# Attention fused with two graph layers on one core: scores behind the outputs, fill between the outputs' parts, and half of the output sum ahead of the maximum

## Chip, cores and metric

One core of a Trainium2 chip runs the whole program. The metric is device time in microseconds, the median of several runs. Engines: PE is TensorE (PEld its weight load), DVE is VectorE, ACT is ScalarE, POOL is GpSimd, SP is SyncE, which issues the DMAs.

## What is computed

The input is x of 32 batches of 512 x 512 and a matrix adj of 512 x 512 with about 3% nonzero entries. Two layers follow each other, each with a layernorm over a residual:

```python
# layer 0
y = einsum('nm,bmd->bnd', adj, x)
x = layernorm(x + y @ weight + bias)
# layer 1: 8 heads of 64, masked by adj == 0
q, k, v = split(x @ w_qkv)
attn = softmax(where(adj == 0, -inf, (q @ k.T) * scale))
o = (attn @ v) @ w_proj + b_proj
x = layernorm(x + (o + (layernorm(o) * ln_gamma + ln_beta)))
```

All is float32. The kernel splits each operand into a rounded high part and the rest (`_hi`, `_lo`) and multiplies hi by hi, hi by lo and lo by hi, so a product costs three matmuls.

## The kernel before

The program has two stages. Layer 0 runs first for all 32 batches and leaves its result in DRAM. The attention stage then runs batch after batch; this is where the change is. A batch has 16 steps (`STEPS`), numbered k. Four steps in a row form a pair: two heads (`PAIRS` is 4), each step handling 128 of the 512 query rows of both heads. A pair's number is also called group.

The scores of step k go through this chain. PE computes them (`scores`, L800) into two banks. DVE adds the mask and finds the row maximum (`masked_max`, L1114). ACT takes the exponent and the row sums (`exponent`, L1013). DVE takes the reciprocal (`inverse`, L1123). POOL multiplies (`normalise`, L728 and L731). PE turns the probabilities in 16 transposes (`turn`, L816). ACT copies the result as pt_hi (L1020) and DVE subtracts to get pt_lo (L1131). This chain is spread over several steps: around the turn of step k, DVE takes the reciprocal for k+1 and the maximum for k+2, ACT the exponent for k+2, POOL normalises k+1, and PE makes the scores of k+3.

When the four steps of a pair are turned, PE multiplies them with v. This is `attend_v` (L840), in four parts of eight matmuls: pt_hi run 0, pt_hi run 1, pt_lo run 1, pt_lo run 0. Each run needs the end of the one before it on the same banks (`pv_half`). The two output banks hold their halves on different partitions, so ACT copies one part of them (`ot_halves`, L1036 and L1037) and DVE adds the other (`ot_sum`, L1149, two instructions on 64 partitions each, the first on partitions 0 to 63). These run in the first step of the next pair.

PE's time between these is filled with other products in units of two simultaneous matmuls (`qk_matmuls`, `v_matmuls`, `project`: L849 and L851). A pair has 48 units. `EARLY` says how many of the next pair's units are issued already in this pair's third step (the first number) and fourth step (the others); `FILL` gives, for the first three steps, the units ahead of the scores and behind them. Pair 0 fills with v, pair 1 with the projection of the batch before, pairs 2 and 3 with q and k of the next batch. Units 24 to 47 of each pair write the output banks, `g_bank[2]` and `g_bank[3]`, which are `o_bank`: unit 24 stands right behind the turn of the second step and waits for both instructions of `ot_sum` (`ot_summed`, L876, L897, L917).

Every engine works its instructions off in the order in which the program lists them. `ready_to_turn` (L805) is PE's wait for the normalised probabilities of the next step and for the pt_lo that frees the turn's banks. In the first three steps it stands ahead of the last fill unit; at the end of a pair it stands ahead of the last matmuls of the last output part.

POOL and ACT also handle the rows of the finished batch at fixed steps (`O_STEP`, `Z_STEP`, `S_STEP`): ACT's `scaled` (L1049) and `result` (L1054), POOL's `scale` (L749), `add_z` (L753, L756) and `power` (L737), DVE's statistics (L1157 to L1162) and `row_shift` (L1167).

Of the kernel before, what the change touches and what calls it, by code (L numbers as in the profile page):

```python
# [31 lines left out]
def graph_layers(nc, x, adj, w0, b0, wqkv, wproj, bproj, gamma, beta, out):  # L32
    B, N, D = x.shape
    T = N // P
    HEAD = 64
    PAIRS = D // (2 * HEAD)
# [15 lines left out]
    with ExitStack() as whole:  # L52
# [483 lines left out]
        with ExitStack() as second:  # L536
# [13 lines left out]
            pt_lo = sb("pt_lo", [P, 2, T, N], F32R)  # L550
# [26 lines left out]
            STEPS = PAIRS * T  # L577
# [59 lines left out]
            S_STEP = [9, 11, 13, 15]  # L637


            EARLY = (4, 6, 2)  # L640
            FILL = ((8, 4), (12, 4), (8, 0))
            assert sum(EARLY) == 12 and sum(EARLY) + sum(map(sum, FILL)) == 48
            BEFORE = [sum(EARLY) + sum(map(sum, FILL[:n])) for n in range(T - 1)]
            assert BEFORE[1] + FILL[1][0] == 36
# [140 lines left out]

            @block.tensor
            def _(pe):
                def scores(b, k):

                    pair, n = k // T % PAIRS, k % T  # L790
                    if n == 0:
                        pe.wait_ge(qklo_made, (b + k // STEPS) * 8 + (2 * pair + 2))
                    parts = ((q_hi, k_hi), (q_hi, k_lo), (q_lo, k_hi))

                    if not (isinstance(b, int) and b * STEPS + k == 0):
                        pe.wait_ge(max_found, b * 32 + 2 * k)
                    for i, (l, r) in enumerate(parts):
                        for a in range(2):
                            h = slice(a * HEAD, (a + 1) * HEAD)
                            last = pe.matmul(s_bank[a][:], l[h, pair, n * P:(n + 1) * P], r[h, pair, :],  # L800
                                             start=i == 0, stop=i == 2)
                            if i == 2:
                                last.then_inc(scores_made, 1)
# [14 lines left out]
                                if a == 1 and m == T - 1:  # L818
                                    last.then_inc(probs_turned, 1)

                def attend_v(b, p, part, run):

                    first, end = part is pt_hi and run == 0, part is pt_lo and run == 0
                    if part is pt_hi and run == 0:
                        pe.wait_ge(pthi_made, b * 32 + (8 * p + 8))
                    elif part is pt_hi:
                        pe.wait_ge(pv_half, b * 16 + (4 * p + 2))
                    elif run == 1:
                        pe.wait_ge(ptlo_made, b * 32 + (8 * p + 8))
                    else:  # L830
                        pe.wait_ge(pv_half, b * 16 + (4 * p + 4))
                    for m in range(T):
                        if end and m == T - 1:
                            if p < PAIRS - 1:
                                ready_to_turn(b, 4 * p + 4)
                            elif not (isinstance(b, int) and b == B - 1):
                                ready_to_turn(b + 1, 0)
                        for a, h in ((run, TOP), (1 - run, BOTTOM)):
                            w = v[h, m, 2 * p + a, :, :].rearrange("p s d -> p (s d)")
                            last = pe.matmul(o_bank[a][:], w, part[h, a, m, :], start=first and m == 0,  # L840
                                             stop=end and m == T - 1)
                            if m == T - 1 and end:
                                last.then_inc(pv_done, 1)
                            elif m == T - 1 and part is (pt_hi, pt_lo)[run]:
                                last.then_inc(pv_half, 1)
# [85 lines left out]
                def batch(b, last_part=True, more=True):  # L931
                    def fill(group, first, count):
                        if group == 0:
                            v_matmuls(b, first, count)
                        elif group == 1 and last_part:
                            project(b, first, count)
                        elif 2 <= group < PAIRS and more:
                            qk_matmuls(b + 1, 48 * (group - 2) + first, count)
                        elif group == PAIRS and more:
                            v_matmuls(b + 1, first, count)  # L940

                    def step(k, group, part):
                        filled = group == 0 or (last_part if group == 1 else more)
                        begin, (front, back) = BEFORE[part], FILL[part]
                        turn(k)
                        fill(group, begin, front)
                        if k + 3 < STEPS or more:
                            scores(b, k + 3)
                        if part == 2:
                            group, begin, front, back = group + 1, 0, 0, EARLY[0]  # L950
                            filled = group < PAIRS and (last_part if group == 1 else more) or group == PAIRS and more

                        if filled:
                            fill(group, begin + front, back - 1)
                        ready_to_turn(b, k + 1)
                        if filled:
                            fill(group, begin + front + back - 1, 1)

                    def last_step(k, group):
                        turn(k)  # L960
                        fill(group + 1, EARLY[0], EARLY[1])


                        if group == 0:
                            pe.wait_ge(vlo_made, b * 4 + 4)
                        elif group == 1 and last_part:
                            pe.wait_ge(o_made, b * 4)
                        elif group >= 2 and more:
                            pe.wait_ge(qklo_made, b * 8 + (4 * group + 4))
                        else:  # L970
                            pe.wait_ge(ot_summed, b * 8 + 2 * group)
                        attend_v(b, group, pt_hi, 0)
                        if k + 3 < STEPS or more:
                            scores(b, k + 3)
                        attend_v(b, group, pt_hi, 1)
                        attend_v(b, group, pt_lo, 1)
                        fill(group + 1, EARLY[0] + EARLY[1], EARLY[2])
                        attend_v(b, group, pt_lo, 0)

                    for group in range(PAIRS):  # L980
                        for part in range(T - 1):
                            step(T * group + part, group, part)
                        last_step(T * group + T - 1, group)
# [25 lines left out]
            def _(act):  # L1009
# [53 lines left out]

                def batch(b, last_part=True, more=True):
                    for k in range(STEPS):
                        pt_hi_part(b, k)
                        if output_at(b, k, 0) and (last_part or k >= T):
                            ot_halves(*output_at(b, k, 0))
                        if k % T == 1:
                            unit_hi(b, k, 0, more)  # L1070
                            unit_hi(b, k, 1, more)
                        if k + 2 < STEPS or more:
                            exponent(b, k + 2)
                        if k % T == 2:
                            unit_hi(b, k, 2, more)
                            unit_hi(b, k, 3, more)
                        if output_at(b, k, 1) and (last_part or k >= T):
                            ot_hi_part(*output_at(b, k, 1))
                        for n in rows_at(k, Z_STEP) if last_part else ():
                            scaled(b, n)  # L1080
                        for batch_row in rows_done(b, k, 2, last_part):
                            result(*batch_row)
# [26 lines left out]
            def _(dve):  # L1109
# [32 lines left out]
                    dve.tensor_tensor(v[:, n, :, 1, :], g_bank[n][:].rearrange("p (h d) -> p h d", d=HEAD),  # L1142
                                      f32(v[:, n, :, 0, :]), ALU.subtract).then_inc(vlo_made, 1)

                def ot_sum(b, p):
                    for a in range(2):
                        dve.wait_ge(ot_half, b * 8 + (2 * p + a + 1))
                        h = slice(a * HEAD, (a + 1) * HEAD)
                        dve.tensor_tensor(ot[h, :], o_bank[a][h, :], ot[h, :], ALU.add).then_inc(ot_summed, 1)  # L1149
# [53 lines left out]
                def batch(b, last_part=True, more=True):  # L1203
                    for k in range(STEPS):
                        group, part = divmod(k, T)
                        ahead = k + 2 < STEPS or more


                        if k + 1 < STEPS or more:
                            inverse(b, k + 1, before_max=ahead)  # L1210
                        if ahead:
                            masked_max(b, k + 2, waited=True)
                        pt_lo_part(b, k)
                        if output_at(b, k, 0) and (last_part or k >= T):
                            ot_sum(*output_at(b, k, 0))
                        for n in rows_at(k, Z_STEP) if last_part else ():
                            row_shift(b, n, 0)
                        if output_at(b, k, 2) and (last_part or k >= T):
# [64 lines left out]
```

## Time and profile before

| | us |
|---|---|
| median of 3 runs | 3403.73 |
| lowest and highest run | 3402.18, 3408.43 |
| profiled execution | 3408.55 |
| its span, first to last instruction | 3406.7 |
| layer 0 | up to about 770 |
| one batch of the attention stage | 80.3 |

The busy share of each engine in the span is PE 98%, PEld 81%, DVE 79%, ACT 65% and POOL 54%. The granted clock of PE is 0.989 of full speed over the span and 1.00 in the attention stage. Durations of matmuls are modelled: one of 512 columns is shown with 0.39 us though the next one starts 0.23 us later, so times between starts say more than durations. In the timeline the first number is the start in us from the span's start, the second the time from the first start to the last end of a merged row.

### The profile page before, as it was taken

The page shows a single profiled execution, that of the slowest core. Times are in us where ns is not written, and L with a number is a line of the kernel's source. Part 1 is how long each engine was busy: PE and PEld are TensorE (multiplying, and loading weights), DVE is VectorE, ACT ScalarE, POOL GpSimd, SP SyncE. Part 2 cuts the span into 40 slices and gives each one's busy share as a digit, 9 for nine tenths or more (in the row PEclk, how much of TensorE's full clock was granted, in tenths as well). Part 3 has the DMA queues.
Part 4 walks back from the last instruction along what each step waited for, and adds up shares of the span by engine and source line. Part 5 has one row for each costly group of instructions (what it writes and reads, how often), then busy time and mean ns, then how long its engine had stood idle before and what let it go on. Part 6 is the DMA issues. An engine that isn't in the chain of part 4 may idle for free.

```text
span 3406.7 us, 87775 instructions
## 1 busy us (share of the span) xinstructions
PE 3326.9 (98%) x31760; PEld 2761.2 (81%) x31760; DVE 2683.6 (79%) x6557; ACT 2211.3 (65%) x4629; POOL 1831.5 (54%) x2559
## 2 busy tenths in 40 slices
PE   7999999998999999999999999999999999999995
PEld 6888888886888888888888888888888888888884
DVE  7666666665788888888888888888888888888886
ACT  4444444434677777777777777777777777777774
POOL 4555555542355555555555555555555555555555
PEclk9999999998999999999999999999999999999997
DMA  5565565562111111111221111111111111122110
GB/s 188 170 197 176 172 194 179 172 189 80 29 54 51 54 51 51 51 51 56 68 67 52 51 51 51 54 51 53 51 51 53 51 51 51 51 67 67 57 38 35
DMA packets 345168, 279.61 MB, mean 82 GB/s; under 512 B 13664, under 2 KB 275808, under 8 KB 344928
## 3 DMA queue, kind: packets, MB, share of 16 engines
q1 hardware_dynamic: 344928, 275.83, 26.6%
q8 instruction: 222, 3.64, 0.5%
q14 instruction: 18, 0.15, 0.0%
HBM read 141.56 MB, written 134.22 MB: 81 GB/s over the span
## 4 chain that ended last, share of the span: by engine, by line
PE 65%; issue 15%; DVE 10%; POOL 9%; ACT 0%; SPq 0%; POOLq 0%; DMA 0%; DVEq 0%
PE bank L849 34%; PE bank L840 14%; PE bank L800 8%; PE bank L816 6%; POOL xb L302 5%; DVE ot L1149 4%; POOL ub L296 4%; DVE pt_lo L1131 3%; DVE probs L1114 2%; PE bank L851 1%; DVE inv_sums L1123 1%; DVE bias_row L1114 0%; PE bank L339 0%; POOL rstd L307 0%; DMA x_lo<-ut_lo 0%
## 5 line engine op out<-in xcount | busy, mean ns | idle before, releaser
L1020 ACT ACTIVATE pt_hi<-bank 128x512 fp32r<-128x512 f32 x1024 | 556.9, 596 | 663.8 <-PE bank L816 648.8
L1013 ACT ACTIVATE probs<-probs,bias_row 128x512 f32<-128x512 f32 x1024 | 733.9, 725 | 16.9 <-DVE bias_row L1114 8.3
L731 POOL TENSOR_SCALAR probs<-probs,inv_sums 128x480 f32<-128x480 f32 (+1 forms) x1024 | 688.9, 686 | 0.0
L1114 DVE CUSTOM_DVE_ANT_0 probs<-bank,mask_bias 128x512 f32<-128x512 f32 x1024 | 661.5, 684 | 8.3 <-PE bank L800 4.1
L1131 DVE TENSOR_TENSOR pt_lo<-bank,pt_hi 128x512 fp32r<-128x512 f32 x1024 | 657.4, 684 | 2.0 <-ACT pt_hi L1020 2.0
L728 POOL TENSOR_TENSOR probs<-probs,inv_sums 128x32 f32<-128x32 f32 x512 | 123.7, 242 | 832.5 <-DVE inv_sums L1123 832.5
L849 PE MATMUL bank<-x_hi,w_hi 64*128 64x512 f32 x1024 | 413.0, 403 | 13.4 <-DMA x_lo<-ut_lo 5.7
L851 PE MATMUL bank<-x_hi,w_hi 64*128 64x512 f32 x1024 | 413.2, 403 | 0.0
L849 PE MATMUL bank<-x_lo,w_hi 64*128 64x512 f32 x1024 | 409.9, 400 | 0.0
L851 PE MATMUL bank<-x_lo,w_hi 64*128 64x512 f32 x1024 | 409.7, 400 | 0.0
L816 PEld LDWEIGHTS bank<-ident,probs 64*128 64x128 f32 x8192 | 338.8, 139 | 74.1 <-POOL probs L731 6.7
L849 PE MATMUL bank<-x_hi,w_lo 64*128 64x512 f32 x1024 | 397.9, 389 | 0.0
L851 PE MATMUL bank<-x_hi,w_lo 64*128 64x512 f32 x1024 | 397.7, 388 | 0.0
L1123 DVE RECIPROCAL inv_sums<-sums 128x2 f32<-128x2 f32 x512 | 83.6, 163 | 350.6 <-PE bank L816 337.7
L816 PE MATMUL bank<-ident,probs 64*128 64x64 f32 x8192 | 339.6, 223 | 7.7 <-DVE pt_lo L1131 5.0
L391 ACT ACTIVATE u<-res,shift,rstd 128x512 f32<-128x512 f32 x128 | 104.5, 817 | 308.4 <-DVE shift L474 308.4
L840 PE MATMUL bank<-pt_hi,v 64*128 64x512 f32 x2048 | 296.4, 404 | 5.2 <-ACT pt_hi L1020 5.1
L749 POOL TENSOR_TENSOR t<-t,gamma_row 128x512 f32<-128x512 f32 x124 | 160.6, 1295 | 233.8 <-ACT t L1049 233.8
L840 PE MATMUL bank<-pt_lo,v 64*128 64x512 f32 x2048 | 280.5, 389 | 0.3
L307 POOL TENSOR_TENSOR rstd<-var_eps,half_neg 128x1 f32<-128x1 f32 x128 | 95.9, 750 | 338.2 <-DVE var_eps L469 338.2
L840 PEld LDWEIGHTS bank<-pt_hi,v 64*128 64x128 f32 x2048 | 208.2, 186 | 49.5 <-issue 34.3
L849 PEld LDWEIGHTS bank<-x_hi,w_hi 64*128 64x128 f32 x1024 | 189.5, 185 | 56.4 <-DVE ot L1149 14.1
(108 smaller groups left out, 10763.6 us busy)
## 6 DMA issues: line engine op xcount, KB each, us to landing
x_in<-in_x_dram SPq DMA_DIRECT2D x32, 1024.0 KB, 5.2
u_beta_rows<-ub SPq DMA_DIRECT2D x32, 1024.0 KB, 4.4
ut_hi<-ut_hi_sb SPq DMA_DIRECT2D x128, 256.0 KB, 4.1
ut_lo<-ut_lo_sb SPq DMA_DIRECT2D x128, 256.0 KB, 3.8
x_hi<-ut_hi SPq DMA_DIRECT2D x128, 256.0 KB, 4.4
x_lo<-ut_lo SPq DMA_DIRECT2D x128, 256.0 KB, 4.7
out_dram<-o SPq DMA_DIRECT2D x128, 256.0 KB, 3.2
ub_row<-u_beta_rows SPq DMA_DIRECT2D x124, 256.0 KB, 2.7
```

Of the source, the lines that this page charges most:

```text
L302: pool.tensor_tensor(xb[:, j, :], x_in[:, j, :], b0_row[:], ALU.add).then_inc(xb_made, 1)
L731: pool.tensor_scalar(probs[:, k % 2, a, cols], probs[:, k % 2, a, cols], inv_sums[:, k % 4, a:a + 1], 0.0, ALU.mult, ALU.add)\
L749: pool.tensor_tensor(t[:], t[:], gamma_row[:], ALU.mult).then_inc(gamma_done, 1)
L800: last = pe.matmul(s_bank[a][:], l[h, pair, n * P:(n + 1) * P], r[h, pair, :], start=i == 0, stop=i == 2)
L816: last = pe.transpose(t_bank[i][:, cols], probs[h, k % 2, a, m * P:(m + 1) * P], ident[h, h])
L840: last = pe.matmul(o_bank[a][:], w, part[h, a, m, :], start=first and m == 0, stop=end and m == T - 1)
L849: top = pe.matmul(banks[run][:], left[run][TOP], right[run][TOP], start=run == 0 and first, stop=run == 1 and end)
L851: bottom = pe.matmul(banks[1 - run][:], left[1 - run][BOTTOM], right[1 - run][BOTTOM], start=run == 0 and first, stop=run == 1 and end)
L1013: act.activation(probs[:, k % 2, a, :], probs[:, k % 2, a, :], ACT.Exp, bias=bias_row[:, k % 4, a:a + 1], scale=-1.0, accum_out=sums[:, k ...
L1020: act.activation(turned_into(pt_hi, k, i), turned(i), ACT.Copy).then_inc(pthi_made, 1)
L1114: dve.tensor_tensor_reduce(probs[:, k % 2, a, :], s_bank[a][:], mask_bias[:, k % T, :], -SCALE, 3.0e38, ALU.add, ALU.min, bias_row[:, k % ...
L1131: dve.tensor_tensor(turned_into(pt_lo, k, i), turned(i), f32(turned_into(pt_hi, k, i)), ALU.subtract).then_inc(ptlo_made, 1)
```

## The change

On PE: in a pair's fourth step the order was pt_hi run 0, scores of k+3, pt_hi run 1, pt_lo run 1, two fill units, pt_lo run 0. It becomes pt_hi run 0, two fill units, pt_hi run 1, pt_lo run 1, two fill units, pt_lo run 0, scores. `ready_to_turn` moves along: it stands ahead of the last two score matmuls. The two new units come from elsewhere: the third step issues two units of the next pair instead of four and ten of its own ahead of the scores instead of eight; the second step issues two behind its scores instead of four.

On ACT: in the first step of a pair `ot_halves` stands ahead of `pt_hi_part` instead of behind it.

On DVE: in the same step the first instruction of `ot_sum` stands ahead of the reciprocal and the maximum, the second stays behind pt_lo.

```diff
-            EARLY = (4, 6, 2)
-            FILL = ((8, 4), (12, 4), (8, 0))
+            EARLY = (2, 6, 2, 2)
+            FILL = ((8, 4), (12, 2), (10, 0))
...
-                def scores(b, k):
+                def scores(b, k, turn_next=None):
...
                     for i, (l, r) in enumerate(parts):
+                        if i == 2 and turn_next is not None:
+                            ready_to_turn(*turn_next)
...
-                        if end and m == T - 1:
-                            if p < PAIRS - 1:
-                                ready_to_turn(b, 4 * p + 4)
-                            elif not (isinstance(b, int) and b == B - 1):
-                                ready_to_turn(b + 1, 0)
+                        if m == T - 1 and turn_next is not None:
+                            ready_to_turn(*turn_next)
...
                         attend_v(b, group, pt_hi, 0)
-                        if k + 3 < STEPS or more:
-                            scores(b, k + 3)
+                        fill(group + 1, sum(EARLY[:2]), EARLY[2])
                         attend_v(b, group, pt_hi, 1)
                         attend_v(b, group, pt_lo, 1)
-                        fill(group + 1, EARLY[0] + EARLY[1], EARLY[2])
-                        attend_v(b, group, pt_lo, 0)
+                        fill(group + 1, sum(EARLY[:3]), EARLY[3])
+
+                        if k + 3 < STEPS or more:
+                            attend_v(b, group, pt_lo, 0)
+                            scores(b, k + 3, (b, k + 1) if group < PAIRS - 1 else (b + 1, 0))
+                        else:
+                            attend_v(b, group, pt_lo, 0)
...
                     for k in range(STEPS):
-                        pt_hi_part(b, k)
+
                         if output_at(b, k, 0) and (last_part or k >= T):
                             ot_halves(*output_at(b, k, 0))
+                        pt_hi_part(b, k)
...
-                def ot_sum(b, p):
-                    for a in range(2):
+                def ot_sum(b, p, halves=(0, 1)):
+                    for a in halves:
...
+                        summed = output_at(b, k, 0) if last_part or k >= T else None
+                        if summed:
+                            ot_sum(*summed, (0,))
                         if k + 1 < STEPS or more:
                             inverse(b, k + 1, before_max=ahead)
                         if ahead:
                             masked_max(b, k + 2, waited=True)
                         pt_lo_part(b, k)
-                        if output_at(b, k, 0) and (last_part or k >= T):
-                            ot_sum(*output_at(b, k, 0))
+                        if summed:
+                            ot_sum(*summed, (1,))
```

## Rows read from the trace of the kernel before

**Rows 1.** The page, part 1: busy time, share of the span and instructions

```profile
PE 3326.9 (98%) x31760; PEld 2761.2 (81%) x31760; DVE 2683.6 (79%) x6557; ACT 2211.3 (65%) x4629; POOL 1831.5 (54%) x2559
```

**Rows 2.** Windows, turn to turn: length, busy PE, PEld, DVE, ACT, POOL, clock, DMA

```profile
2007.39:2011.37 3.98, 3.98 (x48) 3.41 (x46) 3.22 (x9) 3.17 (x7) 2.07 (x4) 1.00 0.00 0
2011.37:2016.55 5.18, 5.15 (x56) 4.14 (x54) 4.66 (x11) 5.08 (x12) 1.57 (x3) 1.00 0.01 3
2016.55:2020.55 4.00, 4.00 (x48) 3.29 (x46) 3.21 (x9) 3.51 (x9) 1.56 (x3) 1.00 0.65 203
2020.55:2027.40 6.85, 6.85 (x72) 5.89 (x70) 3.66 (x9) 2.80 (x7) 1.56 (x3) 1.00 1.00 293
...
2031.41:2036.64 5.23, 5.14 (x57) 4.14 (x55) 5.10 (x11) 3.11 (x8) 1.57 (x3) 1.00 0.00 0
...
2051.49:2056.74 5.25, 5.16 (x57) 4.15 (x55) 5.11 (x12) 5.12 (x12) 2.82 (x4) 1.00 0.16 50
```

**Rows 3.** Timeline of PE and PEld in the first pair's first step

```profile
2006.47 1.09 PE L840 MATMUL bank<-pt_lo,v 64*128 64x512 f32 x8
...
2009.78 0.40 PE L800 MATMUL bank<-k_hi,q_hi 64*128 64x512 f32 x2
...
2012.06 0.18 PEld L849 LDWEIGHTS bank<-w_hi,x_hi 64*128 64x128 f32 x1 [0.17 <-DVE ot L1149]
...
2012.40 0.40 PE L849 MATMUL bank<-w_lo,x_hi 64*128 64x512 f32 x1
```

**Rows 4.** Waits of the whole span: who waited for whom, total us, times, longest

```profile
PEld bank L849 <- DVE ot L1149: 26.8, 124, 0.3
```

**Rows 5.** Timeline of DVE in the same step and into the next

```profile
2008.12 0.17 DVE L1123 RECIPROCAL inv_sums<-sums 128x2 f32<-128x2 f32 x1 [2.16 <-PE bank L816]
2008.20 0.67 DVE L1114 CUSTOM_DVE_ANT_0 probs<-bank,mask_bias 128x512 f32<-128x512 f32 x1
...
2009.41 1.28 DVE L1131 TENSOR_TENSOR pt_lo<-bank,pt_hi 128x512 fp32r<-128x512 f32 x2
2010.61 1.40 DVE L1149 TENSOR_TENSOR ot<-bank,ot 64x512 f32<-64x512 f32 x2
2012.04 0.21 DVE L1167 TENSOR_SCALAR o_shift<-o_mean_var,o_rstd 128x1 f32<-128x1 f32 x1
2012.18 0.17 DVE L1123 RECIPROCAL inv_sums<-sums 128x2 f32<-128x2 f32 x1
2012.38 0.69 DVE L1114 CUSTOM_DVE_ANT_0 probs<-bank,mask_bias 128x512 f32<-128x512 f32 x1
```

**Rows 6.** Timeline of ACT and PEld ahead of the outputs of a fourth step

```profile
2001.28 1.09 ACT L1020 ACTIVATE pt_hi<-bank 128x512 fp32r<-128x512 f32 x2 [0.49 <-PE bank L816]
...
2002.47 0.79 PEld L840 LDWEIGHTS bank<-pt_hi,v 64*128 64x128 f32 x8 [0.25 <-issue]
```

**Rows 7.** Timeline at the kernel's end, where ACT and DVE wait for the outputs

```profile
3373.00 1.21 PE L840 MATMUL bank<-pt_lo,v 64*128 64x512 f32 x8
...
3374.28 0.59 ACT L1036 ACTIVATE ot<-bank 64x512 f32<-64x512 f32 x1 [2.88 <-PE bank L840]
...
3374.90 0.59 ACT L1037 ACTIVATE ot<-bank 64x512 f32<-64x512 f32 x1
3374.91 0.68 DVE L1149 TENSOR_TENSOR ot<-bank,ot 64x512 f32<-64x512 f32 x1 [4.35 <-ACT ot L1036]
```

**Rows 8.** Timeline of DVE between the second pair's second and third step

```profile
2037.02 0.15 DVE L1162 TENSOR_SCALAR o_var_eps<-o_mean_var 128x1 f32<-128x1 f32 x1
...
2037.43 0.17 DVE L1123 RECIPROCAL inv_sums<-sums 128x2 f32<-128x2 f32 x1 [0.25 <-PE bank L816]
```

**Rows 9.** Timeline of ACT and POOL around the third pair's third step

```profile
2056.09 0.82 ACT L1049 ACTIVATE t<-o,o_shift,o_rstd 128x512 f32<-128x512 f32 x1
...
2056.99 1.29 POOL L749 TENSOR_TENSOR t<-t,gamma_row 128x512 f32<-128x512 f32 x1 [2.67 <-ACT t L1049]
...
2058.47 1.35 POOL L731 TENSOR_SCALAR probs<-probs,inv_sums 128x480 f32<-128x480 f32 x2
```

More of the change, by code:

```diff
@@ L819, in turn, with attend_v @@
                                     last.then_inc(probs_turned, 1)
-                def attend_v(b, p, part, run):
+                def attend_v(b, p, part, run, turn_next=None):
                     first, end = part is pt_hi and run == 0, part is pt_lo and run == 0
```

## Prediction, made before the changed kernel was run

> **What bounds the kernel now.** I began with the page. PE is busy for 3326.9 of 3406.7 us and no other engine is above 79% [rows 1], so only idle PE time and waits inside its stream can be won. Both kernels have the same matmuls. Next I cut one batch of the attention stage into its steps, from one step's turn (16 transposes, L816) to the next one's. The start of a turn is called T below, and the four steps of a pair first to fourth. In the first pair they last 3.98, 5.18, 4.00 and 6.85 us [rows 2]. PE loses time in the second. It holds four fill units more than the third (16 against 12). Units are issued 0.23 us apart (the outputs are eight matmuls in four slots: 1.09 less one matmul's 0.40, by three [rows 3]), so without a wait the second step would last 4.00 + 4 x 0.23 = 4.92. It lasts 0.26 more in the first pair, 0.31 in the second and 0.33 in the third (the fourth repeats the third): 1.23 us in a batch. The waits name the cause: 124 waits of PE's weight load for DVE's ot [rows 4], which is 31 batches of four. In the timeline, ot_sum's two halves end at 2010.61 + 1.40 = 2012.01 and the first weights behind the turn are loaded at 2012.06; the next unit comes at 2012.40, and one unit back from that is 2012.17 [rows 3, 5]. So the second step starts its fill when the DVE chain of the first step is done: reciprocal, two maxima, two pt_lo, two halves of ot_sum, from T+0.73 to T+4.62.
>
> **The change, part by part.** Times are against the profiled run: 3408.55 us with a span of 3406.7, so 1.85 lie around the span; the median of the runs is 3403.73, and I take the difference off that.
>
> Fill. Two units leave the second step's back and go to the fourth step: PE issues as many in a pair as before. If nothing waits, the second step lasts 4.00 + 2 x 0.23 = 4.46, the third 4.00, the fourth 6.85 + 0.46 = 7.31. The units between the fourth step's turn and its outputs stay six, so the small wait there for pt_hi stays too: pt_hi ends at 2001.28 + 1.09 = 2002.37, the weights load at 2002.47 [rows 6]. By itself this costs nothing; what it does to DVE and POOL comes below. The two units that now stand between the first two output parts, where six score matmuls stood, give 0.46 us of cover for the last matmuls of the first part (0.40 each): zero. If that cover fell short it would be by less than 0.1 a pair.
>
> Scores last. The six score matmuls are three slots, 0.68 us, so the outputs end that much earlier before the next turn. They end now at 2006.47 + 1.09 = 2007.56, which is T+0.17 [rows 3]; then at T-0.51. The scores are read by the next step's maximum, which waits for that step's turn anyway, and they are made ahead of it: zero. Their own wait, for a maximum of this step, ends long before.
>
> ACT, halves ahead of pt_hi. ACT starts a half 0.07 after the outputs' end (3373.00 + 1.21 = 3374.21, then 3374.28 [rows 7]) and two halves take twice 0.62. So they start at T-0.44, where ACT has nothing to do (2.80 us busy in the fourth step [rows 2]), and pt_hi starts at T+0.80, 0.07 later than now. Its reader, pt_lo, is at T+2.0 (2009.41 [rows 5]): zero.
>
> DVE, first half ahead of the reciprocal. It can start 0.04 after ACT's half (3374.28 + 0.59, then 3374.91 [rows 7]): T-0.44 + 0.59 + 0.05 = T+0.20. DVE is idle there; what queues behind this new wait is the reciprocal and the maxima. A DVE instruction that waits for nothing starts 0.60 after its forerunner (two pt_lo take 1.20 until ot [rows 5]), so the reciprocal starts at T+0.80, against T+0.73 here and T+0.79 in the other pairs. The maximum that frees the banks for the first step's scores is found 1.37 later (2008.12 to 2009.41 and 0.08), at T+2.17; the scores are issued at 2009.78 = T+2.39 [rows 3]. I take 0.02, 0.01, 0.01 and 0.01, so 0.05 a batch. The second half then ends at T+4.12 instead of T+4.62; PE's fill, without its wait, would start at 2012.17 - 0.26 = T+4.52: **the 1.23 us of waits go.**
>
> The Trainium skill has a rule on that spacing ("VectorE: DVE Perf Modes", section "Two Vector instructions with no wait between them"): an instruction that starts in another 32-partition quadrant than the last one is held until all earlier ones have ended. The trace agrees as far as it shows this: the pair of ot halves takes 1.40, not 1.28, and the shift behind them starts only after their end [rows 5]. By the rule a first half followed by the reciprocal, all from partition 0, is not held (0.60). The same page's section "The DRAIN you can't avoid" lets the next instruction wait for an empty pipe (0.70); the sum would then be that of the second rival below.
>
> What is late next. With 0.8 us less in the second step, the engines that only just kept up there are behind in the third, and PE's last unit of the third step stands behind a wait for that step's pt_lo and for the next normalised rows. **DVE, second pair** (T2: the second step's turn): it works until var_eps at 2037.02 = T2+5.61, with room for the next instruction 0.10 later. It gains 0.12: its first maximum is 0.20 behind the reciprocal (2012.18 to 2012.38) where that of the first step is 0.08 behind (2008.12 to 2008.20) [rows 5], and what holds it up, work that ends late in the first step, goes. So the third step's reciprocal starts at T2+5.59 (now 2037.43 = T2+6.02, after 0.25 idle [rows 8]), and pt_lo ends 2.57 later (2008.12 to 2010.69 [rows 5]) at T2+8.16. From a releaser's end to the matmul I take 0.21: 0.10 to the weights [rows 6] and 0.11 from them to the effective start (2012.06 to 2012.17 [rows 3]). The fourth step's turn comes one unit later: 8.16 + 0.21 + 0.23 = 8.60, against 4.46 + 4.00 = 8.46: +0.14. **POOL, third and fourth pair:** ACT reaches the scaled row t at 2056.09 = T2+4.60 and can't be earlier, since its chain starts with the turn; POOL multiplies it from 2056.99 and normalises until 2058.47 + 1.35 = 2059.82 = T2+8.33 [rows 9]. Turn at 8.33 + 0.44 = 8.77: +0.31, twice. DVE, by the sum above with its 0.1 more work, ends there at 8.3, just inside. ACT, busy 5.12 of 5.25 us there [rows 2], is up to 0.8 late for pt_hi; the wait above gives most of it back, but for about 0.04 in the fourth pair (an estimate). The first pair has no such row work: zero.
>
> Sum for a batch: -1.23 + 0.05 + 0.14 + 0.62 + 0.04 = -0.38 us. Times 31: -11.8. The profiled run would be 3396.8, **the median 3392.0.** Steps without fill, in the first and last batch, I leave at zero.
>
> Bounds. A release 0.11 instead of 0.21 in three places: -0.68 x 31 = -21 (3383). The reciprocal 0.70 behind the half instead of 0.60: +0.36 a batch (second rival).
>
> **The rivals.**
> *All of it is won.* If POOL's and DVE's third step has more air than I read, only -1.23 x 31 = -38 stands: 3366. For it: POOL is busy 54% of the span and DVE 79%. Against: both chains above start with a turn and have no gap.
> *Nothing measurable.* The reciprocal is 0.70 behind the half, at T+0.90, the maximum is found at T+2.27 and the scores are 0.09 late in each of four pairs: -0.38 + 0.36 = -0.02, no difference: 3403. For it: every ot half in the trace of before has 0.70 behind it. Against: each of them changes the partitions.
> *Slower.* The first half is a new wait at the head of DVE's queue. If, besides the 0.70, the maximum follows the reciprocal by 0.20, as behind the ot halves now, it starts at T+1.10, the second is found at T+2.39 and the scores come at T+2.60, 0.21 late: +0.84 a batch, less the 0.38 and the 0.05 already counted: +0.41 x 31 = +13: 3417. The place is the scores of each first step; it decides from 0.10 a pair (0.38 by four). Against: the half runs 0.6 us, in which the waits behind it can be worked off.
> *It does not do what it says:* the second half still ends after T+4.5. That needs a chain 0.4 longer than counted, comes only with the rival before and lies in its chance.
>
> **How the numbers follow.** Forecast 0.50, with an own range of 3383 to 3400; all won 0.12; nothing measurable 0.22; slower 0.16. 0.2% is 6.8 us, about what a measurement of this kernel tells from no change, so faster means below 3397. Faster: 0.46 + 0.12 = 0.58; same: 0.04 + 0.21 = 0.25; slower: 0.01 + 0.16 = 0.17. The range leaves out the far half of both outer cases: 3370 to 3415.
>
> **What would show it.** In the profile after: PE's waits for ot gone or under 2 us. The second step 4.4 to 4.5. The third step 4.00 in the first pair, 4.1 to 4.2 in the second, 4.3 in the third and fourth, with PE waiting for pt_lo in the second and for POOL's probs in the others. The fourth step 7.3. The first step at most 4.02; were it 4.1 or 4.2, one of the last two rivals is right. The reciprocal 0.60 behind the half. The prediction is wrong if the third steps stay at 4.00, or if the wait for pt_hi ahead of the outputs grows past 0.1 because ACT's delay is not given back.

## The result and the profile after

The changed kernel is slower by a quarter of a per cent: 3415.07 us (11 runs, 3411.14 to 3420.89) against 3407.6 us for the kernel before, run beside it (11 runs); the ratio is 1.0025 with an interval of 1.0016 to 1.0034. The median of 3403.73 from which the prediction started came from three of these eleven runs. The spans of the profiled executions say the same: 3414.3 and 3406.7 us, +7.6. The forecast of 3392, a gain of 11.8, had the wrong sign, and the result lies at the upper end of the range, just outside it (3415).

The page after, part 1, reads like the one before (PE busy 98%, DVE 79% [rows 1]). The windows from turn to turn show where the time moved. Columns as in [rows 2]: length, busy PE, PEld, DVE, ACT, POOL. The first four lines are the second pair's four steps, the last two the third pair's second and third step.

```profile
2033.24:2037.24 4.00, 4.00 (x48) 3.35 (x46) 3.79 (x9) 3.22 (x8) 1.56 (x3) 1.00 0.64 180
2037.24:2041.67 4.43, 4.43 (x52) 4.11 (x50) 3.70 (x10) 2.52 (x6) 1.57 (x3) 1.00 0.02 4
2041.67:2046.07 4.40, 4.30 (x49) 3.47 (x47) 4.25 (x12) 2.61 (x6) 2.08 (x4) 1.00 0.02 4
2046.07:2053.42 7.35, 7.35 (x76) 6.36 (x74) 6.04 (x17) 4.09 (x9) 3.91 (x6) 1.00 0.00 0
...
2057.45:2061.88 4.43, 4.43 (x52) 3.69 (x50) 3.71 (x11) 3.71 (x9) 2.81 (x4) 1.00 0.25 59
2061.88:2066.39 4.51, 4.41 (x48) 3.21 (x46) 4.10 (x12) 4.18 (x10) 3.45 (x6) 1.00 0.00 0
```

The second step has become short and smooth (5.23 to 4.43). The third, 4.00 before, has PE idle again and lasts 4.40 and 4.51. The wait of 124 times for ot [rows 4] is gone. In its place stands a wait at the last fill unit of the third step. This is the waits view over 1000 to 3300 us (who waited for whom, total, times, longest):

```profile
PEld bank L849 <- POOL probs L732: 43.3, 86, 0.5
PEld bank L840 <- issue: 27.4, 115, 0.3
PEld bank L803 <- DVE bias_row L1119: 23.5, 86, 0.3
```

Its second line, the outputs' first weights behind pt_hi, was there before as well (28.9 us in 114 waits). The name in its first line is misleading. Here is the second pair from its second step's turn (2037.24) to its fourth step's in the timeline, DVE first, then POOL, PEld and PE's turn:

```profile
2038.04 0.17 DVE L1128 RECIPROCAL inv_sums<-sums 128x2 f32<-128x2 f32 x1 [0.70 <-PE bank L819]
...
2039.46 1.28 DVE L1136 TENSOR_TENSOR pt_lo<-bank,pt_hi 128x512 fp32r<-128x512 f32 x2
2040.66 1.28 DVE L1179 TENSOR_TENSOR o<-bank,bproj_row 128x512 f32<-128x512 f32 x2
2041.86 0.68 DVE L1162 BATCH_NORM_STATS2 o_stats<-o 128x6 f32<-128x512 f32 x1
2042.64 0.18 DVE L1165 BATCH_NORM_AGGREGATE o_mean_var<-o_stats 128x2 f32<-128x6 f32 x1
2042.86 0.15 DVE L1167 TENSOR_SCALAR o_var_eps<-o_mean_var 128x1 f32<-128x1 f32 x1
2043.02 0.17 DVE L1128 RECIPROCAL inv_sums<-sums 128x2 f32<-128x2 f32 x1
2043.11 0.68 DVE L1119 CUSTOM_DVE_ANT_0 probs<-bank,mask_bias 128x512 f32<-128x512 f32 x1
...
2044.32 1.28 DVE L1136 TENSOR_TENSOR pt_lo<-bank,pt_hi 128x512 fp32r<-128x512 f32 x2
...
2043.83 1.34 POOL L732 TENSOR_SCALAR probs<-probs,inv_sums 128x480 f32<-128x480 f32 x2
...
2045.72 0.18 PEld L849 LDWEIGHTS bank<-x_lo,w_hi 64*128 64x128 f32 x1 [0.50 <-POOL probs L732]
...
2046.07 0.65 PE L819 MATMUL bank<-ident,probs 64*128 64x64 f32 x15
```

POOL's probs were ready at 2043.83 + 1.34 = 2045.17, but PE loaded at 2045.72. What ended just before that is pt_lo: 2044.32 + 1.28 = 2045.60. `ready_to_turn` waits for both, and the one that came last was DVE's. From its reciprocal behind the second step's turn on, DVE waits for no other engine in this stretch: the third step's reciprocal follows the row work of the second step directly, where before it had 0.25 of idle [rows 8]. The third pair is alike: pt_lo ends at 2064.65 + 1.28 = 2065.93, POOL at 2064.41 + 1.35 = 2065.76, the load comes 0.12 after pt_lo, and the turn at 2066.39.

```profile
2064.65 1.28 DVE L1136 TENSOR_TENSOR pt_lo<-bank,pt_hi 128x512 fp32r<-128x512 f32 x2
...
2064.41 1.35 POOL L732 TENSOR_SCALAR probs<-probs,inv_sums 128x480 f32<-128x480 f32 x2
...
2066.05 0.18 PEld L849 LDWEIGHTS bank<-x_lo,w_hi 64*128 64x128 f32 x1 [0.50 <-POOL probs L732]
```

The scores' wait in the third line is the same delay, met once more within that step: the scores stand ahead of its last units and wait for a maximum.

### The profile page after: what moved, and what is told of

It is laid out like the page before. It is cut to its first block, busy times and chain, and to the rows that moved or that the text cites. A ratio compares the mean times of both kernels' runs of the same rounds, so it can differ in the third digit from the quotient of the medians.

```text
span 3414.3 us, 87775 instructions
## 1 busy us (share of the span) xinstructions
PE 3336.6 (98%) x31760; PEld 2780.2 (81%) x31760; DVE 2696.0 (79%) x6557; ACT 2195.9 (64%) x4629; POOL 1831.8 (54%) x2559
## 4 chain that ended last, share of the span: by engine, by line
PE 76%; issue 13%; POOL 9%; DVE 1%; ACT 0%; SPq 0%; POOLq 0%; DMA 0%; DVEq 0%
PE bank L849 29%; PE bank L840 14%; PE bank L851 14%; PE bank L803 11%; PE bank L819 7%; POOL xb L302 5%; POOL ub L296 4%; PE bank L339 0%; DVE probs L1119 0%; POOL rstd L307 0%; DVE pt_lo L1136 0%; ACT pt_hi L1024 0%; DMA x_lo<-ut_lo 0%; POOLq L299 0%; SPq L77 0%
## 5 line engine op out<-in xcount | busy, mean ns | idle before, releaser
L849 PE MATMUL bank<-x_hi,w_lo 64*128 64x512 f32 x1024 | 410.9, 401 | 0.0
L851 PE MATMUL bank<-x_hi,w_lo 64*128 64x512 f32 x1024 | 410.8, 401 | 0.0
L849 PE MATMUL bank<-x_lo,w_hi 64*128 64x512 f32 x1024 | 404.4, 395 | 6.0
L851 PE MATMUL bank<-x_lo,w_hi 64*128 64x512 f32 x1024 | 406.0, 397 | 0.0
L819 PEld LDWEIGHTS bank<-ident,probs 64*128 64x128 f32 x8192 | 346.9, 139 | 63.0 <-POOL probs L732 6.7
L1154 DVE TENSOR_TENSOR ot<-bank,ot 64x512 f32<-64x512 f32 x256 | 176.4, 689 | 250.6 <-ACT ot L1040 246.6
L1040 ACT ACTIVATE ot<-bank 64x512 f32<-64x512 f32 x128 | 76.3, 596 | 327.6 <-PE bank L840 327.6
```

The costliest lines, as they stand in the source:

```text
L819: last = pe.transpose(t_bank[i][:, cols], probs[h, k % 2, a, m * P:(m + 1) * P], ident[h, h])
L849: top = pe.matmul(banks[run][:], left[run][TOP], right[run][TOP], start=run == 0 and first, stop=run == 1 and end)
L851: bottom = pe.matmul(banks[1 - run][:], left[1 - run][BOTTOM], right[1 - run][BOTTOM], start=run == 0 and first, stop=run == 1 and end)
```

## The experiments

**Theory A**: from the second step's turn on, DVE runs one unbroken chain (reciprocal, maxima, pt_lo, what the fill's products leave to DVE, a row's statistics, then reciprocal, maxima and pt_lo of the third step). It takes 8.8 to 8.9 us until PE may turn again. Before, second plus third step lasted 9.2 us, so the chain fitted; now PE would be done in 8.44, and the chain sets the pace. **Theory B**: the moved halves on ACT and DVE cause the new wait. **Theory C**: POOL's normalisation does, as the waits view says. **Theory D**: the loss lies in the rearranged fourth step.

The table gives the sum of the four pairs' steps in one batch, as the mean of 27 batches between starts of turns. The runs are described below it.

```
                     first   second   third   fourth   batch
before               15.97    20.88   16.01    27.40   80.27
after                16.05    17.74   17.41    29.32   80.51
e1_pe_only           16.03    18.92   16.51    29.30   80.76
e2_sum_only          18.57    19.54   16.43    27.35   81.89
e3_stats64           16.04    17.76   16.51    29.29   79.60
e4_before_shift1     17.36    20.47   15.41    27.39   80.64
e5_first_11          15.43    18.65   16.72    29.25   80.05
e6_stats_third       15.42    18.66   16.55    29.35   79.97
e7_swapped_halves    16.89    17.74   17.03    29.28   80.94
e8_before_stats64    16.02    20.71   16.01    27.37   80.10
```

### PE's part alone

```diff
-                        if summed:
-                            ot_sum(*summed, (0,))
...
-                            ot_sum(*summed, (1,))
+                            ot_sum(*summed)
```

and on ACT `pt_hi_part` ahead of `ot_halves` again.

> The change's PE part alone (scores last, fill between the outputs' parts, two units moved from the second to the fourth step), with ACT and DVE in the order of before. Theory A (DVE's chain from the second step's turn to the third step's pt_lo is one unbroken piece and sets the end of the third step): the wait for ot returns in the second steps (4.77 instead of 4.43), and the third steps shrink by the same amount where DVE set them, so that second plus third stay at 8.83 in the second pair and 8.94 in the third and fourth; only the first pair loses 0.33. A batch 80.8 us, time 3407.6 + 0.5 x 31 = 3423. Theory B (the moved ot_sum half and ACT's halves cause the third step's wait): third steps back at 4.00, time below the changed kernel's 3415.

Measured: 3427.01 us (3424.17 to 3428.05), ratio 1.0061 (1.0045 to 1.0076). The second pair's second and third step:

```profile
2041.22:2045.97 4.75, 4.68 (x52) 3.79 (x50) 4.59 (x11) 3.13 (x8) 1.56 (x3) 1.00 0.00 0
2045.97:2050.07 4.10, 4.10 (x48) 3.29 (x46) 3.95 (x11) 2.61 (x6) 2.08 (x4) 1.00 0.02 4
```

The wait for ot is back (0.32), and the third step has shrunk by the same: together 4.75 + 4.10 = 8.85, after the change 4.43 + 4.40 = 8.83. The means over the batches are 8.83 and 8.83 for the second pair, 8.95 and 8.94 for the third, 8.98 and 8.94 for the fourth. So in these three pairs the removal of the ot wait won next to nothing (0.04 at most); only the first pair, which has no statistics in its second step, keeps its 0.24. Theory B falls: without the moved halves the third steps still last 4.08 to 4.24 in the last three pairs, and the kernel is slower still.

### ACT's and DVE's part alone

```diff
+                        if summed:
+                            ot_sum(*summed, (0,))
                         if k + 1 < STEPS or more:
                             inverse(b, k + 1, before_max=ahead)
```

with ACT's halves ahead of pt_hi, and PE as before.

> The change's ACT and DVE part alone, PE in the order of before. The outputs end at T+0.17, so the first half of the sum can only start at T+0.87 and the reciprocal, 0.60 behind, at T+1.47; the scores of the first step are issued at T+3.05 instead of T+2.39. Theory A: first steps 4.65 instead of 4.00, second steps 4.91 without a wait for ot, third 4.00, fourth 6.85: +0.33 a pair, +41 us, 3449. Rival (the first step has slack for it): within 10 us of before, 3408 to 3418.

Measured: 3462.63 us in one run, 14 more than expected. The first steps last 4.60 to 4.68 (4.65 was expected) and the second 4.88 without a wait for ot. The third steps of the last two pairs are 4.18 where 4.00 was expected, and with smaller amounts elsewhere the batch is 0.3 longer than computed. The trace shows the same DVE chain there: in the fourth pair pt_lo ends 8.48 after the second step's turn, as in the changed kernel, and the scores of the third step, four units ahead of the next turn, wait for that chain's maximum. The run shows what the scores at the end are for: without them the half starts 0.68 later and takes the reciprocal with it.

```profile
2015.05 0.68 DVE L1150 TENSOR_TENSOR ot<-bank,ot 64x512 f32<-64x512 f32 x1 [1.02 <-ACT ot L1036]
2015.66 0.15 DVE L1124 RECIPROCAL inv_sums<-sums 128x2 f32<-128x2 f32 x1
```

### Less statistics on DVE, after and before

The edit takes a row's statistics over 64 of its 512 columns and leaves out the rest of the row, so the kernel computes something else; each of these DVE instructions is 0.47 us shorter. It goes into both kernels.

```diff
-                    dve.bn_stats(stats[:, n, i, :], rows_of).then_inc(stats_made[i], 1)
+                    dve.bn_stats(stats[:, n, i, :], rows_of[:, 0:64]).then_inc(stats_made[i], 1)
```

> The changed kernel with the attention stage's row statistics taken over 64 of 512 columns, so each is some 0.47 us shorter on DVE (one of them stands in the second step of the second, third and fourth pair). Theory A (DVE sets the third steps): the second pair's third step falls from 4.40 to 4.00 and those of the third and fourth pair from 4.51 to 4.31, where POOL's chain takes over: -0.78 a batch, 3415 - 24 = 3391. Theory C (POOL's normalisation, which the waits name, sets them): they stay at 4.40 and 4.51, 3415.

> The kernel before with the same statistics over 64 of 512 columns. Theory A: before the change this DVE work lay beside PE's; the wait was for ot, whose chain holds no statistics. Third steps 4.00 and second steps 5.2 as before, time within 5 us of 3406. Theory C (DVE's total load counts): faster by 10 to 25 us, as in the changed kernel.

Measured, in the changed kernel: 3388.18 us (3385.52 to 3389.04), ratio to the kernel before 0.9943 (0.9928 to 0.9958); the changed kernel with full statistics has 1.0025, so the edit is worth 0.8%, 28 us (24 were expected). The second pair's third step is 3.99, those of the third and fourth 4.26. In the kernel before: 3403.28 us, ratio 0.9996 (0.9986 to 1.0005), no difference, third steps 4.00. Its trace has a batch 0.17 shorter, in the second steps, which would be 5 us and is at the edge of what the times resolve. The same saving of DVE work is worth 28 us in one kernel and nothing that can be measured in the other: before the change it lay beside PE's work, after it on the path. That is theory A, and it speaks against a mere matter of DVE's load (theory C in the second expectation above; in the list of theories C is POOL).

In the third pair of the changed kernel with fewer statistics another engine takes over, near the price that the prediction had computed for it: the turn is at 8.69 where 8.77 was computed. This is its third step, DVE, POOL, PEld:

```profile
2052.22 1.28 DVE L1136 TENSOR_TENSOR pt_lo<-bank,pt_hi 128x512 fp32r<-128x512 f32 x2
...
2052.44 1.33 POOL L732 TENSOR_SCALAR probs<-probs,inv_sums 128x480 f32<-128x480 f32 x2
...
2053.83 0.18 PEld L849 LDWEIGHTS bank<-x_lo,w_hi 64*128 64x128 f32 x1 [0.41 <-POOL probs L732]
```

Now pt_lo is done at 2053.50 and POOL at 2053.77, and the load comes 0.06 after POOL. Here the waits view names the right engine; with the full statistics it named the same one and was wrong. Theory C holds only behind A.

### One unit later for the banks, in the kernel before

```diff
-            EARLY = (4, 6, 2)
-            FILL = ((8, 4), (12, 4), (8, 0))
+            EARLY = (3, 6, 2)
+            FILL = ((8, 4), (13, 4), (8, 0))
```

> The kernel before with one fill unit moved from its third step's back to its second step's front: the third step issues three units of the next pair instead of four, so every unit of the next pair is one place later and the first unit that needs the output banks is the second one behind the second step's turn. Theory A: the wait for ot shrinks by a unit, from 0.26 to 0.33 to 0.03 to 0.10; the second steps are 4.95 in the first pair and 5.22 at most in the others, the third steps 3.8 (a unit shorter, but bound by pt_lo at about 3.81). Second plus third 8.8 to 9.03 instead of 9.18 to 9.25: -0.2 to -0.3 a pair, -25 to -35 us, 3375 to 3383. Rival (the second step is bound by DVE as a whole, not by the place of the unit that waits): no change, 3408.

Measured: 3422.15 us, ratio 1.0045 (1.0031 to 1.0059): a miss. The second steps (5.12; 4.95 was expected in the first pair and at most 5.22 in the others) and third steps (3.85) together win 0.25 a pair, and the wait for ot is gone. But the first steps grew from 4.00 to 4.34. With eleven early units, unit 11 and unit 12 stand side by side behind the turn, and unit 12 begins the second run on its banks and waits for the first run's end (`g % 12 == 0` in `qk_matmuls`, `v_matmuls` and `project`). First the largest new wait of the view over 1000 to 3300 us (17 more have L848 as the releaser, so 114 in all), then PE in the first pair's second step, for comparison, and in the second pair's first step:

```profile
PEld bank L848 <- PE bank L850: 37.6, 97, 0.4
...
2021.55 0.47 PE L848 MATMUL bank<-w_hi,x_lo 64*128 64x512 f32 x1
...
2021.87 0.39 PE L848 MATMUL bank<-w_hi,x_hi 64*128 64x512 f32 x1
...
2037.37 0.47 PE L848 MATMUL bank<-w_hi,ot_lo 64*128 64x512 f32 x1
...
2037.93 0.49 PE L848 MATMUL bank<-w_hi,ot_hi 64*128 64x512 f32 x1
...
2038.27 0.39 PE L848 MATMUL bank<-w_lo,ot_hi 64*128 64x512 f32 x1
```

0.56 from unit 11 to unit 12 where 0.32 is usual right behind a turn (2021.55 to 2021.87), and the restart costs another 0.1 (2037.93 to 2038.27). The kernel before has twelve early units, so that the turn stands between units 11 and 12; here there are eleven.

### Eleven units in the first step

```diff
-            FILL = ((8, 4), (12, 2), (10, 0))
+            FILL = ((8, 3), (13, 2), (10, 0))
```

on the changed kernel.

> The changed kernel with one fill unit moved from its first step's back to its second step's front. Theory A (second plus third step can't be shorter than DVE's chain, 8.83 us in the second pair and 8.95 in the third and fourth, and the first step's last unit waits for pt_lo, which is ready at T+3.4): the first step falls from 4.01 to 3.8 to 3.9, the second grows to 4.66, and in the last three pairs the third shrinks by the same 0.23, since second plus third stay where they are. A batch 80.05 to 80.2 against 80.5: 3401 to 3405. Theory D (the time lies in the rearranged fourth step or in the number of PE's switches): second plus third grow by 0.23 in every pair, and the batch stays at 80.5, 3415.

Measured: 3400.73 us (3397.56 to 3404.42, 11 runs), ratio to before 0.999 (0.9981 to 0.9999). A batch lasts 80.05. The first step is 3.83 to 3.88, the second 4.66, and second plus third are 8.82, 8.94 and 8.95 in the last three pairs, as after the change with one unit less. In the first pair, which DVE does not bind, second plus third grew from 8.43 to 8.66. Theory D falls: it expected the batch to stay at 80.5. The fourth step is unchanged and the gain comes where A puts it. By the two ratios this version is 0.35% or 12 us faster than the changed kernel, and 0.1% faster than the one before, with an interval that only just leaves 1 out. The spans of the profiled runs are 3399.7 and 3406.7.

### One row's statistics moved to the third step

```diff
-            O_STEP = [5, 7, 7, 11]
+            O_STEP = [6, 7, 7, 11]
```

on the version with eleven units.

> As the run with eleven units in the first step, and the statistics of the first row, 1.1 us of DVE work that stood in the second pair's second step, moved to its third step. Theory A: the second pair's second plus third step fall to PE's own 8.66 from 8.83, its fourth step grows by up to 0.1 (pt_lo ready at T+4.2), other pairs unchanged: -0.1 to -0.17 a batch against that run, 3 to 5 us. Theory D: no difference to that run.

Measured: 3401.52 us, ratio 0.999 (0.9981 to 0.9999), no difference to the run before it that the times can tell. In the trace the second pair behaves as expected: its third step falls from 4.16 to 4.00 and its fourth grows from 7.30 to 7.40. The batch is 0.08 shorter, 2 us, and that is below what the runs resolve.

### The halves swapped

```diff
-                            ot_sum(*summed, (0,))
+                            ot_sum(*summed, (1,))
...
-                            ot_sum(*summed, (1,))
+                            ot_sum(*summed, (0,))
```

with ACT's two copies swapped to fit.

> The changed kernel with the sum's two halves swapped on ACT and DVE: the half of partitions 64 to 127 stands ahead of the reciprocal, that of partitions 0 to 63 behind pt_lo. If the change of partitions is what puts 0.20 instead of 0.08 between the reciprocal and the first maximum of the second step: the gap moves to the first step (reciprocal 0.70 behind the half, maximum 0.20 behind the reciprocal, first step 4.2), the second step has 0.08, and second plus third fall by 0.1 in the last three pairs: +0.4 to +0.5 a batch, 3428 to 3432. If it is something of the second step itself, its 0.20 stays and the first steps stay at 4.01: 3415.

Measured: 3432.01 us in one run. DVE around a first step of the swapped kernel:

```profile
2041.06 0.69 DVE L1154 TENSOR_TENSOR ot<-bank,ot 64x512 f32<-64x512 f32 x1 [3.83 <-ACT ot L1040]
2041.79 0.17 DVE L1128 RECIPROCAL inv_sums<-sums 128x2 f32<-128x2 f32 x1
2041.98 0.69 DVE L1119 CUSTOM_DVE_ANT_0 probs<-bank,mask_bias 128x512 f32<-128x512 f32 x1
...
2045.87 0.17 DVE L1128 RECIPROCAL inv_sums<-sums 128x2 f32<-128x2 f32 x1 [0.79 <-PE bank L819]
2045.95 0.68 DVE L1119 CUSTOM_DVE_ANT_0 probs<-bank,mask_bias 128x512 f32<-128x512 f32 x1
```

Behind the half of partitions 64 to 127 the reciprocal starts 0.73 later and the maximum 0.19 behind it. In the second step, now behind the half of partitions 0 to 63, the maximum is 0.08 behind the reciprocal. Below is the changed kernel in the same places:

```profile
2033.42 0.68 DVE L1154 TENSOR_TENSOR ot<-bank,ot 64x512 f32<-64x512 f32 x1 [3.85 <-ACT ot L1040]
2034.03 0.17 DVE L1128 RECIPROCAL inv_sums<-sums 128x2 f32<-128x2 f32 x1
2034.11 0.68 DVE L1119 CUSTOM_DVE_ANT_0 probs<-bank,mask_bias 128x512 f32<-128x512 f32 x1
...
2038.04 0.17 DVE L1128 RECIPROCAL inv_sums<-sums 128x2 f32<-128x2 f32 x1 [0.70 <-PE bank L819]
2038.23 0.69 DVE L1119 CUSTOM_DVE_ANT_0 probs<-bank,mask_bias 128x512 f32<-128x512 f32 x1
```

There it is 0.61 and 0.08 in the first step and 0.19 in the second. So the gap of 0.2 belongs to the half on the upper partitions and moves with it. First steps of 4.18 to 4.27 and second plus third shorter by 0.12 to 0.13 in the last three pairs follow, and the batch of +0.43 against the changed kernel.

## Why the prediction was wrong, step by step

**The bound and the wait: right.** The wait for ot was worth 1.23 us a batch; the second steps fell from 20.88 to 17.74, which is 3.14, and 1.84 of that is the eight moved units. That leaves 1.30.

**Fill, scores last, ACT, first half: right.** Fourth step 7.33 instead of 7.31. The half starts at 2033.42 = T+0.18 (T+0.20 computed), the reciprocal at T+0.79 (0.80), pt_hi at T+0.79 (0.80). First steps 4.00 to 4.01: +0.07 a batch (0.05 computed). The small cover between the first two output parts was enough. The 0.04 that the sum had for ACT in the fourth pair did not show: in every pair the outputs' first weights are loaded 0.11 after pt_hi and 1.92 after the turn, before and after the change, so what would have shown the prediction wrong there did not happen.

**What is late next: the right place, the wrong size, and this turned the sign.** This is the step that failed: the DVE chain from the second step's turn to the third step's pt_lo was summed too short in all three pairs, and in two of them POOL was named in its place. Third steps were to cost +0.76 a batch and cost +1.40. In the second pair the chain was to reach pt_lo at T2+8.16 and PE's turn at 8.60; it was 8.36 (2045.60 less 2037.24) and 8.83. In the third and fourth pair DVE was to end at 8.3, inside POOL's 8.33; POOL ended at 8.31, but DVE at 8.48, and it became the bound, with the turn at 8.94 instead of 8.77. The waits view names POOL there, as the prediction had said, and read by the name alone it would have confirmed the wrong engine. Three things were missing:

- 0.12: I had the maximum close up on the reciprocal in the second step, because I put the gap of 0.20 in the trace of before down to "work that ends late in the first step". It is still 0.19 after the change. The swapped halves show the real cause, the step from the upper partitions back to partition 0. The Trainium skill ("VectorE: DVE Perf Modes", section "Two Vector instructions with no wait between them"), which the prediction cited for the neighbouring gap, covers this one too: it keeps the last start quadrant for each memory apart, so the reciprocal, which reads no PSUM, does not clear it for the maximum, which does. The two kernels agree with it: 0.19 and 0.08 change places when the halves do. The prediction had shortened the rule to the instruction just before, and used it where it spoke for the change and not where it spoke against it.
- 0.06: the reciprocal stands 0.16 behind var_eps, not 0.10, when nothing is idle between them.
- 0.03: from the end of pt_lo to the turn it is 0.46 to 0.47, not 0.44. (Behind POOL, in the run with fewer statistics, it is 0.40.)

So the turn after the third step came at 8.83, 8.94 and 8.94 where 8.60, 8.77 and 8.77 were computed, 0.57 in all. The other 0.07 of the 0.64 is that PE was done with the second step in 4.43, not 4.46, and waited that much more in the third.

**The sum.** -1.30 + 0.07 + 1.40 + 0.07 = +0.24 a batch, times 31 is +7.4 us; the spans differ by 7.6. That these agree so closely is partly luck: from the first turn to the last the profiled runs differ by 7.0, what lies ahead of the first turn, layer 0 above all, took 3.0 longer, and what follows the last turn 2.4 less. Over the ten profiled runs the first turn comes at 803.2 to 807.2 us, with layer 0 the same in all, so most of these 3.0 is scatter. The forecast was a difference of two large terms, -1.23 and +0.85. An error of about 0.2 us in the chain of three pairs, 2 to 3% of it, is 0.57 a batch and larger than the whole forecast of -0.38.

**The rivals.** "All of it is won" was wrong in every pair but the first. "Slower" had the right sign (+13 where +7.5 was measured), but by a mechanism that did not occur, so the sign is luck: the scores of the first step were not late. Its gap of 0.20 was real, but it sits in the second step. "Nothing measurable" needed 0.70 behind the half; it was 0.61. The forecast's bounds listed a release that was cheaper and a half that was dearer, but put no upper bound on the third step's chain, which is where 0.1 more would have cost 9 us.

## What to carry to other kernels

A wait that is removed from PE's stream pays only until the unbroken chain of another engine becomes the longer one, so add up that chain from a point that PE itself sets (here a turn) to the next point that PE waits for, and compare it with PE's own work between the two: here 8.83 to 8.94 against 9.2 before and 8.44 after. Filler moved out of such a stretch takes away the cover of the chain, even though the number of matmuls stays the same. Where two semaphores stand at one place, compare the ends of both releasers with the start of the waiting load before you believe the name in the waits view.

## What the runs showed of the hardware

A DVE instruction on partitions 64 to 127 starts 0.70 to 0.71 after one that started at partition 0, and the next one from partition 0 starts 0.73 after it, not 0.60 (an `ot` half and its neighbours, before, after and with swapped halves). The first one after that which reads PSUM from partition 0 starts 0.19 to 0.20 behind the reciprocal, not 0.08, even where DVE was idle for 0.70 us ahead of the reciprocal. Where the second run on a pair of banks waits for the first run's end and stands right behind it, PE loses 0.34 us (first steps of 4.34 instead of 4.00).
